# Splitting the first range of columns in two in the last stage of a two-layer kernel

## The reference

```python
x_slice = jnp.take_along_axis(xf, tok_dims, axis=1)          # 16 values a token, of its tile
tok_min = x_slice.min(axis=1); tok_max = x_slice.max(axis=1)
onehot = tile_idx[None, :] == jnp.arange(NUM_TILES)[:, None]
tile_min = jnp.where(onehot, tok_min[None, :], jnp.inf).min(axis=1)    # over all tokens
tile_max = jnp.where(onehot, tok_max[None, :], -jnp.inf).max(axis=1)
mn = tile_min[tile_idx][:, None]; mx = tile_max[tile_idx][:, None]     # the "range" of a token
u = jnp.clip((x_slice - mn) / (mx - mn + 1e-08), 0.0, 1.0 - 1e-06)
gi = jnp.clip((u * GRID).astype(jnp.int32), 0, GRID - 1)               # the "cell"
b = spline_bases[tile_idx[:, None], j, gi]; s = spline_slopes[tile_idx[:, None], j, gi]
delta = (b + s * x_local) * output_scale[tile_idx][:, None]
out = jnp.zeros_like(xf).at[jnp.arange(N)[:, None], tok_dims].set(delta)
...
x = _layernorm(x + _L0_ffn_ref(x, ...), axis=-1)      # here x is y; the sum inside adds it once more
```

## Time and profile before

| what | value |
|---|---|
| median of 3 runs | 1265.76 us (1264.2 to 1268.58) |
| the profiled execution, its own time | 1264.53 us |
| its span in the trace | 1262.8 us |
| DVE busy | 1084.7 us (86%) |
| TensorE busy, mean granted clock | 1111.0 us (88%), 0.926 of full |
| ACT busy | 943.7 us (75%) |
| POOL busy | 818.6 us (65%) |
| DMA | 174.88 MB, mean 138 GB/s |

### The profile page before, as it was taken

The page is one execution under the profiler, slowest core; times in us unless marked ns, Lnnn a source line. Parts: engine busy times, 40 slices in busy tenths (PEclk is TensorE's granted clock), DMA queues, the critical chain, the costliest instruction groups (busy, mean ns, idle before and its releaser), DMA issues. The chain is left out here.

```text
span 1262.8 us, 31497 instructions
## 1 busy us (share of the span) xinstructions
PE 1111.0 (88%) x9278; PEld 714.4 (57%) x9278; DVE 1084.7 (86%) x2538; ACT 943.7 (75%) x1805; POOL 818.6 (65%) x1647
## 2 busy tenths in 40 slices
PE   5799999999999999999999999999999997835510
PEld 4456666666666666666666666666666663421000
DVE  4898888898989898989999898999899977788874
ACT  4757888888888888888888888888888875415863
POOL 3125666676767676767676767676767666534675
PEclk8999999999999999999999999999999998666555
DMA  4112222222222222222222222222222213958999
GB/s 146 34 39 105 107 107 107 107 105 105 105 105 105 105 105 105 105 105 105 104 104 104 96 95 96 103 104 105 105 105 95 95 68 107 396 197 339 407 419 385
DMA packets 63650, 174.88 MB, mean 138 GB/s; under 512 B 11435, under 2 KB 22643, under 8 KB 63606
## 3 DMA queue, kind: packets, MB, share of 16 engines
q1 hardware_dynamic: 52118, 149.33, 31.8%
q10 hardware_dynamic: 5984, 23.07, 4.5%
q0 software_dynamic: 5504, 1.94, 1.0%
HBM read 69.06 MB, written 101.04 MB: 135 GB/s over the span
## 5 line engine op out<-in xcount | busy, mean ns | idle before, releaser
L1190 DVE SCALAR_TENSOR_TENSOR acc<-xT_all,cw_sb,acc 128x256 f32<-128x256 f32 x768 | 354.0, 519 | 6.8 <-ACT acc L849 6.8
L876 ACT ACTIVATE sg<-TS,bet,gam 128x256 f16<-128x256 f32 x244 | 123.3, 556 | 26.7 <-PE TS L493 26.7
L513 PE MATMUL PR<-xT_all,w_sb 128*128 128x256 f32 x512 | 137.3, 392 | 3.4 <-ACT xT_all L812 3.4
L525 PE MATMUL WKB<-w_sb,tS 128*128 128x512 f32 x256 | 137.4, 618 | 0.0
L849 ACT ACTIVATE acc<-xT_all,cb_sb,cw_sb 128x256 f32<-128x256 f32 x256 | 132.5, 591 | 4.9 <-DVE xT_all L1176 2.9
L595 PE MATMUL PR<-shT,w_mg_sb 128*64 128x128 f32 x2048 | 128.8, 280 | 6.6 <-ACT shT L858 6.6
L368 POOL TENSOR_TENSOR AT<-AT,Wm 128x128 f32<-128x128 f32 x210 | 108.0, 514 | 39.5 <-DVE AT L1216 24.8
L567 PE MATMUL OB<-th_all,AT 128*128 128x512 f32 x256 | 123.4, 605 | 5.8 <-DVE AT L368 2.0
L595 PE MATMUL PR<-shT,w_rk_sb 128*64 128x128 f32 x2048 | 125.9, 276 | 0.0
L595 PEld LDWEIGHTS PR<-shT,w_rk_sb 128*64 128x64 f32 x2048 | 110.5, 137 | 25.7 <-issue 25.7
L595 PEld LDWEIGHTS PR<-shT,w_mg_sb 128*64 128x64 f32 x2048 | 113.4, 139 | 19.0 <-issue 12.0
(11 more groups left out here) (274 smaller groups left out, 2744.4 us busy)
## 6 DMA issues: line engine op xcount, KB each, us to landing
xin_all<-in_x SPq DMA_DIRECT2D x32, 1024.0 KB
y_ring<-y_all SPq DMA_DIRECT2D x32, 1024.0 KB, 4.1
y_scratch<-y_all SPq DMA_DIRECT2D x32, 1024.0 KB, 6.1
own<-y_scratch SPq DMA_DIRECT2D x5, 2048.0 KB, 17.1
rows<-y_scratch SPq DMA_DIRECT2D x4, 2048.0 KB, 13.3
out<-rows ACTq DMA_DIRECT2D x8, 1024.0 KB, 18.5
out<-own ACTq DMA_DIRECT2D x6, 1024.0 KB, 18.9
RX<-RE SPq DMA_DIRECT2D x128, 32.2 KB
```

The source lines that it names most:

```text
L513: i = pe.matmul(PR[:, 0:T], w0_sb[:, blk, :], xT[b][:, blk, HIST:HIST + T], start=(blk == 0), stop=(blk == NB - 1))
L525: pe.matmul(WK[h][:], tS[b][:, chunk_cols(c)], w1_sb[:, half_cols(h)], start=True, stop=False)
L876: nc.scalar.activation(sg[:, blk, :], at[:, (blk % 2) * T:(blk % 2 + 1) * T], ACT.Sign, scale=gam[:, blk:blk + 1], bias=bet[:, blk:blk + 1 ...
L1190: v.scalar_tensor_tensor(acc[:, blk, :], xT[b][:, blk, i:i + T], cw_sb[:, blk, i:i + 1], acc[:, blk, :], ALU.mult, ALU.add).then_inc(e_con ...
```

## The change

The first range of columns, (0, 12), becomes two, (0, 4) and (4, 12). TensorE makes both right after one another, the second when DVE has taken out the first, and only then goes on to `last_turned`. On DVE nothing is written differently: `ranges_in` and `cells` of a range stand before the batch that begins where the range begins, so those of columns 0 to 3 stand before batch 0 and those of columns 4 to 11 now stand between batch 0 and batch 1.

```diff
-            RANGES = ((0, 12), (12, 36), (36, NC))
+            RANGES = ((0, 4), (4, 12), (12, 36), (36, NC))
...
                 ranges(*RANGES[0])
+                ranges(*RANGES[1])
                 last_turned()
                 for t in range(EARLY, 6):
                     tables(t)
-                ranges(*RANGES[1])
+                ranges(*RANGES[2])
                 for t in range(6, 12):
                     tables(t)
-                ranges(*RANGES[2])
+                ranges(*RANGES[3])
                 for t in range(12, PAIRS):
                     tables(t)
```

## The result

The changed kernel took 1272.97 us in the median of 4 runs (1269.86 to 1273.89), the kernel before 1264.98. The ratio is 1.005 with a 95% interval of 1.0029 to 1.0071: slower by 0.5%, some 6.3 us (the two medians lie 8.0 us apart; I go by the ratio). I had forecast no change, with a range up to 1268.7.

What follows compares the result with a forecast made beforehand. The last stage was taken as a copy bound by DMA, so only DMA idle time counted: six terms summed to 3.97 us against 4.17, -0.2 us, giving about 1265.5 us from 1265.76, range 1262.8 to 1268.7.

Steps and rivals of the forecast that it cites:

- Batch 0 earlier: Batch 0's first store issued 1.2 us earlier: DVE saves 1.28, TensorE 0.25, POOL's delay costs 0.3.
- DVE's fixed part of 2.59 us: On DVE, the time of `ranges_in` through the four bits that does not depend on columns: 2.59 us, 17 instructions.
- The delay between POOL and DVE: POOL's `moments` of batch 0 beside DVE's `cells` of columns 4 to 11: 0 to 1.19 us later, 0.3 taken.
- TensorE's table at the half clock: TensorE's later table for batch 1 may fall on full or half clock: 0 to 0.86 us, 0.3 taken.
- What hides the lateness: Batches 1 to 5 come 2.6 us late, yet DMA idle time sums to 3.97 us against 4.17.
- Just covered.: Before batch 2's first store, four stores and two slots' loads, 8.4 MB or 20.4 us, keep DMA busy to 1171.
- the last scatter: POOL's last scatter, 2.6 us later, lands at 1262.0, 6.6 us after issue; it decides from 3.4 us lateness on.
- The lateness comes out at the end: slower: Rival: POOL's last scatters or failed DMA cover before batch 2 delay the end; 2 to 2.9 us, 1268.2 us; chance 0.2.
- passing 0.3%: A measurable slowdown would need 3.8 us of lateness all the way through; slower was given 0.05.

Runs made afterwards that it cites:

- the two delays that I tried: Unsplit kernel with POOL's cast later and 8 or 14 idle DVE reductions between batches 0 and 1: +3.4 and +5.7 us against the kernel before.
- the split without the stall: The changed kernel with POOL's cast of in_row moved behind batch 1's scatters, run twice: +3.3 and +2.8 us against the kernel before.
- the loads in the new order: Slot 9's load issued by ACT behind batch 1's fourth store; cast later: split +2.5 us, unsplit with 8 idle DVE reductions +3.4, against the kernel before.

## Why the prediction was wrong

**Batch 0 earlier.** Right: 1.2 us forecast, 1.2 measured, with a little luck: DVE's sums came 1.36 us earlier and not 1.53, and POOL took 0.13 us more and not 0.3; DVE's fixed part of 2.59 us for a second `cells` was right too (3.93 us for 8 columns with the stall taken off, forecast 3.87).

**The delay between POOL and DVE.** This is one of two steps that failed. I asked what DVE's new instructions do to POOL's `moments` (0.3 us taken, 0.13 measured) and cited the rule of an exclusive lock, but did not go on along POOL's queue: behind the coefficients of batch 0 stands the 2.4 us cast of in_row. In the kernel before it ran beside copies out of PSUM and held nobody. Moving 17 instructions from SBUF to SBUF to that place put them under it: 2.2 us of stall, worth 2.8 to 3.0 us at the end.

**TensorE's table at the half clock.** 0.3 us taken, 0.64 measured, inside the bounds I gave (0 to 0.86). That the number fits is luck: the unsplit kernels with the cast moved have the same wait, so it is not shown to be a cost of the split.

**What hides the lateness.** The other step that failed, and the larger one by its kind, in two places. The first is "Just covered." Before batch 2 I counted four stores and two loads, 8.4 MB, as queued. The second of these loads waits for batch 1's last store, and that store, under load, lets the load go not 4 but 11 us after its own issue; the 4.0 us of the earlier trace rows were of a nearly empty queue, and in the trace of the kernel before this very load already came 10.4 us behind its store (stage time 46.0, batch 2's first store at 47.1). Only 6.3 MB was there, 15 us of work for the 20 us. With 0.4 us of spare in my own sum I should have given this rival more than 0.2. The second place is the last scatter, to which I gave 3.4 us of room. I let it land 6.6 us after its end and took that for the end of its chain; in the traces the span ends no less than 10.5 us after its beginning, and in the kernel before it ended 11.0 us after. The room was 0.5 us. What came of both is 0.9 us or more for each us of lateness, with no free part in the two delays that I tried.

**The rivals.** "The lateness comes out at the end: slower" had the right sign, and both of its branches happened. The cover before batch 2 failed (share 0.49 at 63 GB/s). And the last scatter decides: in the changed kernel it began at 1257.35 and the span ended 10.8 us later, 1.5 us after the last traffic; in its repetition these are 10.6 and 1.2 us. That the DMA engines were still full until about 1265 does not speak against it, since both chains are late by nearly the same. The price of 2 to 2.9 us is near the split without the stall (+2.8 and +3.3); the stall makes the rest. I had said that passing 0.3% would need more lateness than the rows give; a 2.4 us instruction on the neighbour's queue gave it.

**What stays open.** How the 3 us divide between the two chains is known by the traces only: a kernel that issues the last scatters earlier, with the loads in the new order, would test it. Why the span goes on for some 4 us after a scatter's 6.6 us to landing, no trace here shows.

## What to carry to other kernels

When instructions move in time, read what the neighbour engine executes in the place they move to, in both directions and along its whole queue, not only the instruction that depends on them. In a stage that copies at full rate, count as queued only what has nothing left to wait for: a load behind a store inherits that store's landing time under load, and this was more than twice its landing time when the queue was empty. Ask of every chain that the end waits for how much room it has, counted from a trace's own end and not from a landing time: when one fix removes a gap and the time stays, the next chain is the first thing to read. An early start of a pipeline is worth little (about 1 us here) when the later batches are what keeps it full.

## What the runs showed of the hardware

A DVE instruction with all its operands in SBUF stood for the whole of a POOL cast of 128 x 1280: 2404 ns instead of 218 for the one-input 8-bit instruction, 2.78 us instead of 0.56 for the two-input one. The same cast beside DVE's copies in PSUM cost nothing that shows (in the kernel before, 0.69 and 0.42 us for the 512 and 256 wide ones, as elsewhere).

A load starts slowly: from 1161 to 1165 us, when the load of slot 9 (issued at 1158.78) began to flow without any pause before it, the DMA share of the changed kernel was 0.93 with only 250 GB/s moved, and from 1170.4 to 1174, behind a pause, the share was 0.49 with 63 GB/s, where 0.49 of a full stretch would be about 200. Some of what I counted as idle time is this.

The end of the span came at least 10.5 us after the beginning of the last indirect store of GpSimd, with no DMA traffic at all in the last 1.9 to 3.2 us of six kernels, and 0.7 to 0.8 us after the last traffic where the row stores ended last.
